# AdaLN block and six attention/FFN layers on one core: a three-pass output product, one buffer for the heads' outputs, Gelu read from PSUM, a new order of the turns

## The reference

```python
q, k, v = split(shift_tokens(x) @ Wqkv[i])            # 128 -> 3 x 1024
q = rotary(l2norm(q) * qs);  k = rotary_inv(l2norm(k) * ks)
attn = softmax(8 * q @ k.T, causal, window of 32)      # sequences of 32 tokens
x = (attn @ v) @ Wo[i] + x                             # 1024 -> 128
xn = layernorm(shift_tokens(x)) * g + b
a, gate = split(xn @ W1[i] + b1)                       # 128 -> 2 x 341
x = (a * gelu(gate)) @ W2[i] + b2 + x
```

## Time and profile before

| | |
|---|---|
| runs | 3024.75 us median of 3 (3023.71 to 3027.78) |
| profiled execution | 3025.93 us, its span 3024.1 us |
| mean granted TensorE clock | 0.986 |
| busy in the span | PE 94%, DVE 79%, ACT 80%, POOL 70% |

### The profile page before, as it was taken

The page is one execution under the profiler, slowest core; times in us unless marked ns, Lnnn a source line. Parts: engine busy times, 40 slices in busy tenths (PEclk is TensorE's granted clock), DMA queues, the critical chain, the costliest instruction groups (busy, mean ns, idle before and its releaser), DMA issues. The chain is left out here.

```text
span 3024.1 us, 90067 instructions
## 1 busy us (share of the span) xinstructions
PE 2847.9 (94%) x34784; PEld 1995.9 (66%) x34976; DVE 2396.9 (79%) x3168; ACT 2423.9 (80%) x3783; POOL 2114.6 (70%) x1517
## 2 busy tenths in 40 slices
PE   8799978999999999999999999999999999999995
PEld 7688856666666666666666666666666666666662
DVE  7899967887787888778788787877788787887872
ACT  5788858788887878888788888878888887888872
POOL 6767657777677777777777777777777776777760
PEclk9899989999999999999999999999999999999997
DMA  1000011100111010010001111000110100100002
GB/s 51 22 1 1 1 33 26 27 23 20 27 32 30 23 26 24 21 41 24 23 23 26 28 31 26 23 23 24 30 31 23 26 23 25 28 21 20 18 21 64
DMA packets 73039, 76.57 MB, mean 25 GB/s; under 512 B 23078, under 2 KB 46692, under 8 KB 72804
## 3 DMA queue, kind: packets, MB, share of 16 engines
q1 hardware_dynamic: 71780, 74.01, 9.5%
q10 hardware_dynamic: 1152, 1.20, 0.1%
HBM read 22.72 MB, written 2.10 MB: 8 GB/s over the span
## 5 line engine op out<-in xcount | busy, mean ns | idle before, releaser
L1313 POOL TENSOR_TENSOR qk_r<-qk_r,qk_t 128x1024 f32<-128x1024 f32 x384 | 917.9, 2391 | 549.9 <-DVE qk_r L1169 387.9
L776 PE MATMUL pa<-w_hi,xs_hi 128*128 128x512 f32 x1152 | 576.2, 500 | 41.1 <-DVE qk_r L1169 24.8
L1162 DVE TENSOR_REDUCE ss<-sq 128x16 f32<-128x1024 f32 x384 | 463.6, 1207 | 19.0 <-ACT sq L959 18.2
L1178 DVE TENSOR_TENSOR qk_t<-pa,rot 128x1024 f32<-128x1024 f32 x384 | 465.5, 1212 | 0.0
L1169 DVE TENSOR_TENSOR qk_r<-pa,rot 128x1024 f32<-128x1024 f32 x384 | 465.5, 1212 | 0.0
L804 PEld LDWEIGHTS px<-ident_sb,qk_r 128*128 128x128 f32 x3072 | 352.3, 141 | 164.6 <-issue 100.5
L776 PE MATMUL pa<-w_hi,xs_lo 128*128 128x512 f32 x1152 | 456.5, 396 | 0.0
L776 PE MATMUL pa<-w_lo,xs_hi 128*128 128x512 f32 x1152 | 454.6, 395 | 0.0
L804 PE MATMUL px<-ident_sb,qk_r 128*128 128x128 f32 x3072 | 402.8, 274 | 30.4 <-POOL qk_r L1322 14.4
L1012 ACT COPY kT<-px 64x1024 f32<-64x1024 f32 x384 | 385.2, 1003 | 34.5 <-PE px L804 29.8
L1322 POOL TENSOR_TENSOR qk_r<-qk_r,inv 128x1024 f32<-128x1024 f32 x192 | 365.9, 1906 | 43.8 <-ACT inv L996 43.5
(11 more groups left out here) (142 smaller groups left out, 5344.4 us busy)
## 6 DMA issues: line engine op xcount, KB each, us to landing
pT<-prT SPq DMA_DIRECT2D x768, 64.0 KB, 2.0
w_part<-in_Wqkv SPq DMA_DIRECT2D x40, 192.0 KB, 2.7
wo<-in_Wo SPq DMA_DIRECT2D x6, 512.0 KB, 4.5
c_h<-in_x SPq DMA_DIRECT2D x4, 512.0 KB, 9.9
o_x<-in_x SPq DMA_DIRECT2D x8, 256.0 KB, 4.8
out<-o_out SPq DMA_DIRECT2D x8, 256.0 KB, 4.3
w<-in_W SPq DMA_DIRECT2D x6, 341.0 KB
spare<-in_Wqkv SPq DMA_DIRECT2D x1, 1536.0 KB, 6.3
```

Of the source, the lines that this page charges most:

```text
L776: last = pe.matmul(pa[(u + c) % 2][:, half * 512:half * 512 + 512], x[:, j * P:(j + 1) * P], w[:, at], start=(k == 0), stop=(k == 2))
L1162: dve.reduce_sum(ss[:, c, :], heads(sq[:]), AX.X).then_inc(s[sum_sem], 1)
L1178: dve.tensor_tensor(halves(qk_t[:, c, :]), halves(pa[(3 * j + c) % 2][:])[:, :, ::-1, :], table.unsqueeze(1).to_broadcast([P, HEADS, 2, DH ...
L1313: pool.tensor_tensor(qk_r[:, j % 2, c, :], qk_r[:, j % 2, c, :], qk_t[:, c, :], ALU.add)\
```

## The change

- The output product takes fp32r operands: `wo` is split into `wo_hi` (ACT, once a layer) and `wo_lo` (POOL, once a layer); the heads' outputs into `oT_hi` (ACT's copy, as before) and `oT_lo`, a new DVE pass for every tile (`rest_of_outputs`). Three products stand for one. PE's `transpose_q` waits for `oT_lo` where it waited for ACT's copy.
- `oT_hi` and `oT_lo` are one group deep; `spare` now holds `v` and `qk_r`.
- The bias, Identity and Gelu of a gate block are one activation out of PSUM; the table sets are loaded in turn 1, before `square_q` and after the third gate block.
- `scale_shift` moves from ACT to DVE. Centring squares straight from PSUM; `fsq`, `frs` and `fn` share one tile `fx`.
- `kT` is laid out by halves; the copies stay ACT's.
- The order of the calls changes on every engine. The first two groups of every layer are written out; POOL computes the next layer's rotary tables and `wo_lo` in group 1, in place of between the layers.
- `wo` of the next layer is asked for in group 4; `w_part` has one buffer.
- Before the first group, the waits for cleared tiles stand at their first use.

The diff, cut; the bodies show the lines of the new order (in DVE's, ACT's and PE's the removed lines are left out), in the order DMA, PE, ACT, DVE, POOL, PE's body:

```diff
-w_part = sb("w_part", [DM, 2, W_PART])
+w_part = sb("w_part", [DM, W_PART])
 wo = sb("wo", [P, HP, DM])
+wo_hi = sb("wo_hi", [P, HP, DM], F32R)
+wo_lo = sb("wo_lo", [P, HP, DM], F32R)
 w1 = sb("w1", [DM, 2 * HID])
...
-qk_r = sb("qk_r", [P, 2, 2, INNER])
+qk_r = spare[:, GT * INNER:2 * GT * INNER].rearrange("p (k c e) -> p k c e", k=2, c=2)
 qk_t = sb("qk_t", [P, 2, INNER])
 qT = sb("qT", [P, HP, P])
-kT = sb("kT", [P, HP, TILE_B, 2, S])
-
-v = sb("v", [P, GT, INNER])
+kT = sb("kT", [P, 2, HP, TILE_B, S])
+
...
-oT = spare[:].rearrange("p (g h t n) -> p g h t n", g=2, h=HP, t=GT)
+oT_hi = sb("oT_hi", [P, HP, GT, P], F32R)
+oT_lo = sb("oT_lo", [P, HP, GT, P], F32R)
...
-new_layer(0)
-body(0, 0, 0)
-body(1, 0, 1)
-with eng.Fori(2, GROUPS) as g:
-    body(g, 0, g)
-for l in range(1, DEPTH):
+for l in range(DEPTH):
     new_layer(l)
-    with eng.Fori(0, GROUPS) as g:
+    for g in range(2):
+        body(g + l * GROUPS, l, g)
+    with eng.Fori(2, GROUPS) as g:
         body(g + l * GROUPS, l, g)
...
-        wait_for(sp, s["w_lo_ready"], k - 1)
-        sp.dma_start(w_part[:, k % 2, :], of("Wqkv", l + 1)[:, c * W_PART:(c + 1) * W_PART])\
+        wait_for(sp, s["w_lo_ready"], k)
+        sp.dma_start(w_part[:], of("Wqkv", l + 1)[:, c * W_PART:(c + 1) * W_PART])\
             .then_inc(s["w_part_loaded"], 16)
 
     def load_scales(l):
...
-        if 0 < l < DEPTH and g == 0:
-            sp.wait_ge(s["wo_done"], i)
-            load_wo(l)
+        if l + 1 < DEPTH and g == 4:
+            sp.wait_ge(s["wo_lo_ready"], l + 1)
+            load_wo(l + 1)
         if 0 < l < DEPTH and g == 1:
...
+    def transpose_q(i, j, back):
+        n, j, live = tile(i, j, back)
+        if live:
+            if isinstance(n, int) and n == 0:
+                pe.wait_ge(s["mask_ready"], 2)
+                pe.wait_ge(s["zeroed"], 7)
             pe.wait_ge(s["rot_q"], n + 1)
-            wait_for(pe, s["pv_out"], n - 2)
+            wait_for(pe, s["oT_lo_ready"], n - 2)
...
+    def project_out(i, back, lo, hi):
+        g, live = group(i, back)
         if live:
             if lo == 0:
-                pe.wait_ge(s["pv_out"], GT * (g + 1))
-                pe.wait_ge(s["wo_loaded"], (g // GROUPS + 1) * 16)
...
+                for k, (w, o) in enumerate(((wo_hi, oT_hi), (wo_hi, oT_lo), (wo_lo, oT_hi))):
+                    last = pe.matmul(pg[:], w[:, hp, :], o[:, hp, :, :].rearrange("p t n -> p (t n)"),
+                                     start=(hp == 0 and k == 0), stop=(hp == HP - 1 and k == 2))
...
+    def gate_gelu(i, back, k):
+        g, live = group(i, back)
         if live:
             m = HBLK[k][1]
             act.wait_ge(s["gate_done"], 3 * g + k + 1)
-            act.activation(gt[0:m, k, :], pg[0:m, :], ACT.Identity, bias=b1[0:m, 1, k:k + 1])\
+            act.activation(gt[0:m, k, :], pg[0:m, :], ACT.Gelu, bias=b1[0:m, 1, k:k + 1])\
...
+    def tables(i, back, name):
+
+        g, live = group(i, back)
+        if live:
+            act.preload_act_table_set(name)
...
+        n, k, live = tile(i, j, back)
+        if live:
             act.wait_ge(s["pv_done"], n + 1)
             if k == 0:
-                wait_for(act, s["wo_done"], g - 1)
-            act.copy(oT[:, bass.ds(g % 2, 1), :, k, :].rearrange("p o h (r q) -> p (o r) h q", r=2),
+                wait_for(act, s["wo_done"], i + (j - back) // GT)
+            act.copy(oT_hi[:, :, k, :].rearrange("p h (r q) -> p r h q", r=2),
...
+    def round_wo(l):
+        act.wait_ge(s["wo_loaded"], 16 * (l + 1))
+        wait_for(act, s["wo_done"], l * GROUPS)
+        act.copy(wo_hi[:], wo[:]).then_inc(s["wo_hi_ready"], 1)
...
     def body(i, l, g):
         for j in range(GT):
+            if isinstance(g, int) and g == 1 and l < DEPTH and j == 0:
+                round_wo(l)
+            copy_v(i, j, 1)
             if j == 1:
+                tables(i, 2, GELU)
+            square_q(i, j, 0)
+            if j == 0:
+                square_centred(i, 2)
+                copy_centred(i, 2)
+            if j == 1:
+                gate_gelu(i, 2, 0)
+            copy_qT(i, j, 1)
+            if j == 1:
+                gate_gelu(i, 2, 1)
+            if j == 0:
+                shift_hi(i, 0, 1)
             if j == 2:
                 round_part(l, g)
+            square_k(i, j, 0)
+            copy_kT(i, j, 1)
             if j == 1:
+                gate_gelu(i, 2, 2)
+                tables(i, 2, EXP_LN)
+            exponentials(i, j, 2)
+            if j == 0:
+                log_variance(i, 2)
+            floor_norms(i, j, 0)
+            if j == 0:
+                inverse_deviation(i, 2)
+            if j == 3:
+                shift_ffn(i, 1)
+            log_norms(i, j, 0)
+            copy_oT(i, j, 3)
+            if j == 1:
                 shift_hi(i, -1, 0)
+            inverse_norms(i, j, 0)
 
...
+    def scale_shift(i, back):
+        g, live = group(i, back)
+        if live:
+            dve.wait_ge(s["ffn_loaded"], (g // GROUPS + 1) * FFN_DMAS * 16)
+            dve.wait_ge(s["fn_mul"], g + 1)
+            dve.tensor_scalar(fx[:], fx[:], ln_par[:, 0:1], ln_par[:, 1:2], ALU.mult, ALU.add)\
+                .then_inc(s["fn_ready"], 1)
+
+    def rest_of_outputs(i, j, back):
+        n, k, live = tile(i, j, back)
+        if live:
+            dve.wait_ge(s["pv_out"], n + 1)
+            dve.tensor_tensor(oT_lo[:, :, k, :].rearrange("p h (r q) -> p r h q", r=2),
+                              px[:].rearrange("p (r h q) -> p r h q", r=2, h=HP),
+                              oT_hi[:, :, k, :].rearrange("p h (r q) -> p r h q", r=2).bitcast(F32), ALU.subtract)\
+                .then_inc(s["oT_lo_ready"], 1)
+
...
     def body(i, l, g):
         for j in range(GT):
+            sum_squares(i, j, 0, 0, "sq_q", "sum_q")
+            times_cos(i, j, l, 0, "sq_q", "tq_done", "cos_q")
+            times_sin(i, j, l, 0, "sq_q", "rot_q", "sin_q")
+            times_cos(i, j, l, 1, "sq_k", "tk_done", "cos_k")
+            sum_squares(i, j, 0, 1, "sq_k", "sum_k")
+            times_sin(i, j, l, 1, "sq_k", "rot_k", "sin_k")
+            if j == 1:
+                gated(i, 2, 0)
+            denominators(i, j, 2)
+            if j == 0:
+                normalise(i, 2)
+            if j == 3:
+                add_attention(i, 1)
+            if j == 0:
+                scale_shift(i, 2)
+            rest_of_outputs(i, j, 3)
+            if j == 1:
+                gated(i, 2, 1)
             if j == 2:
+                add_ffn(i, 2)
+            maximum(i, j, 1)
+            turn_probs(i, j, 2)
+            subtract_maximum(i, j, 1)
             if j == 1:
+                gated(i, 2, 2)
...
+    def rest_of_wo(l):
+        pool.wait_ge(s["wo_hi_ready"], l + 1)
+        pool.tensor_tensor(wo_lo[:], wo[:], wo_hi[:].bitcast(F32), ALU.subtract).then_inc(s["wo_lo_ready"], 1)
...
     def body(i, l, g):
         for j in range(GT):
-            rotate(i, j, 0, "cos_q", "sin_q", "rot_q")
+            if j == 0:
+                shift_lo(i, 0, 0)
+            rotate(i, j, 1, 0, "cos_q", "sin_q", "rot_q")
             if j == 2:
                 shift_lo(i, 0, 1)
+            rotate(i, j, 1, 1, "cos_k", "sin_k", "rot_k")
             if j == 3:
                 rest_of_part(l, g)
-            if j == 3:
-                shift_lo(i, -1, 0)
-            rotate(i, j, 1, "cos_k", "sin_k", "rot_k")
-            norm_probs(i, j)
-            norm_keys(i, j)
-            norm_scores(i, j)
+            norm_probs(i, j, 3)
+            norm_keys(i, j, 1)
+            norm_scores(i, j, 2)
+            if isinstance(g, int) and g == 1 and l < DEPTH and j == 0:
+                rest_of_wo(l)
+            if isinstance(g, int) and g == 1 and l < DEPTH and j == 1:
+                next_tables(l)
...
         for j in range(GT):
+            scores(i, j, 2)
+            if j == 2:
+                a_block(i, 2, 1)
             project_q(i, j, l)
+            if j == 0:
+                subtract_mean(i, 2)
             if j == 1:
+                gate_block(i, 2, 0)
+            transpose_q(i, j, 1)
             if j == 2:
+                a_block(i, 2, 2)
             project_k(i, j, l)
             if j == 3:
+                project_out(i, 1, 0, HP // 2)
+            if j == 1:
+                gate_block(i, 2, 1)
+            transpose_k(i, j, 1)
+            if j == 2:
+                down(i, 2)
+            if j == 0:
+                variance(i, 2)
+            if j == 1:
+                gate_block(i, 2, 2)
             if j == 3:
+                project_out(i, 1, HP // 2, HP)
+            project_v(i, j, l)
+            weigh_values(i, j, 3, 1)
             if j == 1:
+                a_block(i, 2, 0)
```

More of the change, by code:

```diff
@@ L905, in a_block, with down @@
                         at, m = HBLK[k]
-                        pe.matmul(pg[0:m, :], w1[:, at:at + m], fn[:], start=True, stop=True).then_inc(s["a_done"], 1)
-                def down(i):
-                    g, live = group(i, 2)
```

(38 more changed lines are left out.)

329 lines of the change are left out of this document (120 added, 209 removed).

## The result

The changed kernel takes 3038.58 us (median of 5, 3036.13 to 3042.60), the kernel before 3024.75 (median of 5). The ratio is 1.0045, 95% interval 1.0030 to 1.0059: slower by 0.45%. The forecast was 3020. The range held the time, the sign was wrong.

The account below looks back on a forecast made before the run. DVE's turns with their waits for POOL and ACT, not PE, were taken to set the period; 23 - 18 + 3 - 5 - 1 = +2, less 7 for shorter handovers, gave -5 and 3020 us; range 2960 to 3060.

Parts of the forecast that it names:

- The turns: DVE's four turns of a steady group: 53.1 us in sum against 52.6 before, +23 us over 46 groups.
- Rival A: Turn 0's wait for POOL or turn 3's for shift_ffn is absent: 0.9 to 1.3 us a group, 2975; 28%.
- Rival C: The new DVE pass is exposed in one more turn: 1.13 us a group, 3072; 20%.
- Rival B: PE sets the steady group's period and hides every DVE wait: 50.4 us a group, 2905; 4%.
- Rival D: Gelu's table set lacks the squares: four more table loads a group, 246 us, 3266; 3%.
- E: Output product on PE: fp32r is no faster with these operands, PE keeps 51.2 us, forecast unchanged; no chance given.
- The start of a layer: Rotary tables moved into group 1, where POOL is idle: 3.6 us saved five times, -18 us.
- Ends: Drain: Gelu, scale_shift and centring savings less one new pass, twice, -5 us; kernel start, fewer waits for cleared tiles, -1.
- the rest of the sum: Terms outside the drain: steady groups +23, layer starts -18, rounding wo +3, kernel start -1, then 7 off for shorter handovers.

Follow-up runs that it names:

- the first experiment: Changed kernel with ScalarE's shift for the FFN in turn 3 moved behind the copy of the heads' outputs: 3000.64 us, ratio 0.9918.

## Why the prediction was wrong

**The turns were right.** Predicted 12.65, 13.75, 12.7, 14.0; measured 12.46, 13.87, 12.65, 14.10. Their sum, 53.08, is 0.02 from the predicted 53.1. Rival A, that one of the two waits isn't there, is refuted: the scale and shift takes 1.22 behind POOL and 0.55 where POOL is idle, and turn 3 has the 2.70 of idle time. Its price of 0.9 to 1.3 a group fits the order in ACT's list, worth 1.1 in the first experiment; taking away the wait for POOL brought 0.25, with a pass that is 0.26 longer. Rival C decided nothing beyond the turn in which I had it already: without the pass, turns 1 and 2 are no shorter. Rival B fails: even with the pass gone, PE's saving of 1.3 was worth 0.24 in a steady group, and 1.2 only in the last layer. Rival D is refuted by the two table loads of a group, E by the products at 0.23.

One refinement: the last layer has no next weights to round, so its turn 2 is 11.68 and its group 52.1 against 52.24 before. I had counted 0.5 for its groups too, 4 us too much. The first three groups of a layer, in which wo is rounded and weights arrive, are up to 1.1 longer, 5 us in all where I had 3.

**The start of a layer was right.** 18 us predicted. Before, the five groups that reach into the next layer are together 17.7 us longer than their neighbours; in the changed kernel they are as long as their neighbours, and moving only the tables in the kernel before was worth 17.

**The failed step** is this one: "Ends. The drain is serial: the Gelu's 1.48, 0.4 of scale_shift and 0.6 of centring go, one new pass comes, twice: -5." It measured +9.2, which is 14 off: of the 15 us by which the profiled execution lies above its forecast (3036.1 against 3020.9) it is nearly all. Two things are wrong in it.

The smaller: the terms. First, they don't add up to what I wrote: 1.48 + 0.4 + 0.6 less one pass of 1.2 is 1.3, and twice that 2.6, not 5. Second, their sizes, read in the last FFN with TensorE kept at work: from the first `a` product to its gating the changed kernel takes 1.23 us and the one before 2.78, so the separate Gelu cost its 1.5 there; the scale and shift gained 0.25 for 0.4; centring gained 0.1 for 0.6, since the variance product still waits for the copy that ACT makes beside the squares. As the kernels are, at half clock, even the Gelu is mostly hidden: before, the `a` product starts at 2992.44, the Gelu runs beside it from 2993.70 to 2995.18 and the gating starts at 2995.22, and all that gained about 0.6. Third, the 1.3 that the output product saves is on the path here, and I left it out; and so is the order by which add_ffn stands behind the new pass (3.15 us idle at 2975.87, above). At one clock the drain gained some 1.7.

The larger: the term holds nothing for the clock. It takes every product of the drain to be as long after the change as before. With TensorE kept at work, the changed kernel's drain is 18.0 shorter and that of the kernel before 6.1, or 7.1 without the 1.0 that the added products cost there: the 11 between them are the clock. The trace of before had it in plain sight: 0.67, 0.50 and 0.61 in the last three windows of its drain. I never looked at the clock by stretches there.

**Near by luck** was the rest of the sum. Outside the drain I had +7, and took 7 off because "each is as likely to be 0.1 to 0.2 shorter a group"; the trace has +1.1. But no turn was shorter: the group is as long as I had placed it. What came in less were the last layer's 4 and the start, -4.7 (the first two rows of the table) where I had -1. Without the 7 the whole sum would have been nearer: +2, on the right side of zero.

What stays open: why the clock falls earlier. In the 10 us ahead of the first fall (2930.8 to 2940.8) TensorE was busy 8.29 us; in the same stretch of the kernel before it was 8.57, and in a later one (2946.7 to 2956.7) only 5.56, and there the clock stayed. So its busy time just before doesn't tell the two kernels apart. Nor is the fall the same each time: the kernel before with only its tables moved has the same code in the drain and took 100.8 there, against 98.4, and the two versions that differ only in a place of POOL's work took 100.7 and 105.2. These are single executions; that the added products shorten the drain stands on the medians too (17 us in the changed kernel, 6 in the one before). Taking out the pass shortens the drain by three times its own length; that its waits bring the fall is likely, but not shown.

## What to carry to other kernels

A serial tail has to be priced by the clock that it runs at: look at the granted clock by stretches, and if it falls, either shorten TensorE's waits there or give it work that nobody reads (17 us of 3038 here), and look whether that work delays what is read. Try the parts of a change one by one: without the three-pass product and its pass, this one was 22 us faster than the kernel before, with them 14 slower. When an operation that reads a copy is added, follow the copy back in its engine's list: here a shift ahead of it, moved behind it, was worth 38 us, more than the whole change moved. And once TensorE and DVE are both busy for nine tenths of the period, what one turn saves the next can give back: name, for each turn, the engine that is next.

## What the runs showed of the hardware

An elementwise pass of DVE with two scalars per partition took 0.55 us for 512 columns between SBUF tiles with GpSimd idle, 1.22 behind GpSimd's addition, and 0.81 with its source in PSUM, with GpSimd idle and with GpSimd adding alike. An fp32r product of 512 columns took 0.23 at full clock and 0.43 at half. Products that nobody reads, in the idle times of TensorE, held the clock at 1.0 through a tail of 73 us; nine of them in one place of the kernel before delayed its output product by 1.0 us, and in the changed kernel none was seen to delay anything. Without them the clock went between 1.0 and 0.5 several times in the tail, and code that was the same took 98.4 and 100.8 us there.
